# Delta rule attention: the chunk systems stored by column, the solve's operations placed one by one, and another order on all five engines

## The chip, the cores and the metric

One core of a Trainium2 chip runs the whole program. The metric is device microseconds of one execution, the median over runs; lower is better. The kernel runs on five engines with queues of their own: TensorE (PE) for matmuls, VectorE (DVE), ScalarE (ACT), GpSimd (POOL), and SyncE (SP), which here issues the DMAs.

## The reference, cut to what matters

The program is a two-layer decoder (six sub-layers, each followed by a residual sum and a layer norm) on x of shape (2, 2048, 512). The change touches only the first sub-layer, a delta-rule attention with 16 heads of 32 features:

```python
k = _short_conv(x @ Wk.T + bk, wk_conv, bk_conv)   # q and v the same way, 4 taps
beta = jax.nn.sigmoid(x @ Wbeta.T + bbeta)
v = jax.nn.silu(v)
k = k / (knorm + EPS); v = v / (knorm + EPS); q = q / (qnorm + EPS)
def step(S, inp):
    q_t, k_t, v_t, b_t = inp
    pred = jnp.einsum('bhk,bhkv->bhv', k_t, S)
    S = S + b_t[..., None, None] * (k_t[..., None] * (v_t - pred)[..., None, :])
    o_t = jnp.einsum('bhk,bhkv->bhv', q_t, S)
    return (S, o_t)
```

The output is RMS-normalised, goes through `Wo`, is added to x and layer-normed.

## The kernel before, in words

`delta_rule_attention` walks over the sequence in 16 tiles of 128 tokens (both batches at once). Within a tile the recurrence is cut into 4 chunks of 32 tokens. For 32 items (4 head groups x 2 batches x 4 chunks) and the 4 heads in the partitions' quadrants, the triangular 32x32 system of a chunk is inverted in advance, so that the state moves by whole chunks.

A tile n goes through these pieces, each a small function in the code:

- TensorE `project` p = 0 (beta) and 1 to 12 (k, q, v by four groups); ScalarE `keep` (out of PSUM), `first_tap` and `taps` (products of the short convolution); GpSimd `copy_history` and `pair_taps` (L533, sum of two taps); VectorE `join` (L1105, two additions for each of k, q, v), `turn` (L1116, a 32x32 block transpose).
- norms: ScalarE `square` and `take_root`, VectorE `sum_squares` (L1122) and `invert_norms` (L1128 to L1133), GpSimd `rate_keys` (L540) and `mask_beta` (L549).
- the systems: TensorE `keys_keys` (L623), VectorE `mask` (L1143), `to_systems` (L1148: transposes the masked products into `t_sys`), 60 operations `substitute` (L1162 a product, L1165 an addition, each needing the one before), `from_systems` (L1176: transposes back into `tT`), GpSimd `scale_t` (L553).
- the states, for each chunk c: TensorE `predict`, VectorE `miss` (L1186), TensorE `update`, ScalarE `keep_u`, TensorE `step_state`, VectorE `carry` (L1191), then `predict` of the next chunk. `outputs` reads states and `u`.
- the outputs: `square_outputs`, `keep_outputs` (L927), `rms_sum`, `rms_add`, `rms_invert` (L1209 to L1212), `scale_outputs` (L558), `turn_outputs` (L1217), TensorE `project_out` for each batch (L675), VectorE `add` (L1224) and `moments`, `norm.root` on GpSimd, `finish` on ScalarE, `turn_new` and `keep_new`, SP `store`. One PSUM bank, `b_out`, serves `project_out` of both batches and `turn_new`.

The order of the work is written out by hand: on each engine `unrolled` calls `step(n)` for n = 0, 1, ..., and a step names pieces of tile n and of the tiles 1 to 4 before it (`t1` to `t4`). Engines meet only through semaphores, so each engine runs its list strictly in order, and a piece that waits holds all that stand behind it. In the last steps (draining) TensorE and ScalarE also run `next_product` and `keep_next`, first work of the next sub-layer, which otherwise starts when this stage has ended.

The memory that matters: `masked_kq` holds for each of two tile parities, item by item, 32 numbers of the keys' system and 32 of the queries' one after the other. So `to_systems` reads with steps of 64 elements and writes with steps of 32; `from_systems` reads in one run and writes with steps of 32. The products of `substitute` are kept in `squares[:, 0]`, which ScalarE's `square(n, 0)` writes too and therefore waits for the solve.

## Time and profile before

| | |
|---|---|
| median of 3 runs | 2832.5 us (2830.06, 2832.5, 2836.57) |
| span of the profiled execution, first to last instruction | 2826.6 us |
| its own time | not given beside the span; the median lies 5.9 us above the span |
| mean granted TensorE clock | 0.970 of full speed |
| busy over the whole span | PE 90%, DVE 79%, ACT 50%, POOL 18% |
| delta-rule stage | about the first 1041 us of the span |

The page's shares are means over six sub-layers with different limits. The change lies in the first, so the stage's own windows are what counts. "Idle before" in a row of the timeline stands in brackets with the engine that ended it. PE rows of the small matmuls overlap, so a busy PE isn't PE at its peak.

### The profile page before, as it was taken

The page shows a single profiled execution, that of the slowest core. Times are in us where ns is not written, and L with a number is a line of the kernel's source. Part 1 is how long each engine was busy: PE and PEld are TensorE (multiplying, and loading weights), DVE is VectorE, ACT ScalarE, POOL GpSimd, SP SyncE. Part 2 cuts the span into 40 slices and gives each one's busy share as a digit, 9 for nine tenths or more (in the row PEclk, how much of TensorE's full clock was granted, in tenths as well). Part 3 has the DMA queues.
Part 4 walks back from the last instruction along what each step waited for, and adds up shares of the span by engine and source line. Part 5 has one row for each costly group of instructions (what it writes and reads, how often), then busy time and mean ns, then how long its engine had stood idle before and what let it go on. Part 6 is the DMA issues. An engine that isn't in the chain of part 4 may idle for free. (4 is left out here: it accounts for less than half of the span.)

```text
span 2826.6 us, 83010 instructions
## 1 busy us (share of the span) xinstructions
PE 2548.6 (90%) x35304; PEld 1801.5 (64%) x35304; DVE 2224.5 (79%) x4027; ACT 1417.6 (50%) x2569; POOL 512.1 (18%) x661
## 2 busy tenths in 40 slices
PE   6788989899898979999999987997799999989998
PEld 5566666666666756777677654443377777766765
DVE  3898988889998628888887784987778888871886
ACT  7667666777566213323333223545366666651554
POOL 2233322233223210000000000004511111120222
PEclk9999999999999989999999999999899999998999
DMA  2001111111111221121220114548932122123332
GB/s 89 21 16 34 56 34 41 34 34 56 34 41 63 100 97 41 53 75 53 75 68 31 60 60 145 186 158 290 315 118 75 61 61 89 61 75 105 119 121 74
DMA packets 165805, 234.24 MB, mean 83 GB/s; under 512 B 17858, under 2 KB 94018, under 8 KB 162884
## 3 DMA queue, kind: packets, MB, share of 16 engines
q1 hardware_dynamic: 165444, 229.01, 24.6%
q8 instruction: 278, 4.55, 0.7%
q14 instruction: 83, 0.68, 0.1%
HBM read 136.18 MB, written 92.80 MB: 81 GB/s over the span
## 5 line engine op out<-in xcount | busy, mean ns | idle before, releaser
L612 PE MATMUL delta_banks<-both_columns,both_mats 128*128 128x256 f32 x1536 | 383.5, 394 | 5.7 <-ACT both_line L865 4.8
L612 PEld LDWEIGHTS delta_banks<-both_columns,both_mats 128*128 128x128 f32 x1536 | 278.9, 191 | 48.9 <-ACT both_line L865 8.0
L883 ACT ACTIVATE both_product<-both_line,delta_conv_w 128x256 f32<-128x256 f32 x576 | 248.6, 496 | 7.1 <-DVE both_conv L1105 6.2
L1512 PE MATMUL ctxatt_banks<-both_product,ctxatt_oT 128*128 128x512 f32 x512 | 228.4, 599 | 4.9 <-DVE both_conv L1627 4.9
L1473 PE MATMUL ctxatt_banks<-both_line,both_mats 128*128 128x256 f32 x960 | 221.5, 384 | 1.3 <-SPq L1424 1.3
L1473 PEld LDWEIGHTS ctxatt_banks<-both_line,both_mats 128*128 128x128 f32 x960 | 180.5, 193 | 24.8 <-SPq L1424 1.6
L1162 DVE TENSOR_TENSOR delta_squares<-delta_t_sys 128x30 f32<-128x30 f32 (+14 forms) x480 | 175.0, 365 | 12.5 <-issue 0.2
L1165 DVE TENSOR_TENSOR delta_t_sys<-delta_t_sys,delta_squares 128x30 f32<-128x30 f32 (+14 forms) x480 | 165.4, 345 | 16.5
L865 ACT ACTIVATE both_line<-delta_banks,delta_proj_b 128x256 f32<-128x256 f32 x192 | 87.8, 457 | 170.3 <-PE delta_banks L612 170.1
L1512 PEld LDWEIGHTS ctxatt_banks<-both_product,ctxatt_oT 128*128 128x128 f32 x512 | 95.3, 191 | 115.5 <-issue 109.0
L1559 ACT ACTIVATE ctxatt_probsT<-ctxatt_banks 128x512 f32<-128x512 f32 x128 | 69.5, 594 | 189.3 <-PE ctxatt_banks L1494 189.2
L533 POOL TENSOR_TENSOR both_product<-both_product 128x1024 f32<-128x1024 f32 x48 | 116.9, 2437 | 186.8 <-ACT both_product L883 186.8
L675 PE MATMUL delta_banks<-delta_woT,delta_oT 128*128 128x512 f32 x256 | 126.2, 639 | 22.7 <-DVE delta_norm_y L1224 22.7
L2447 PE MATMUL wkv_banks<-wkv_mixed,decay_wkT 128*128 128x256 f32 x512 | 118.3, 386 | 19.1 <-DVE wkv_mixed L2624 11.0
L1105 DVE TENSOR_TENSOR both_conv<-both_conv,both_product 128x1024 f32<-128x1024 f32 x96 | 117.7, 1226 | 19.8 <-POOL both_product L533 15.3
L219 POOL TENSOR_TENSOR ctxatt_norm_var_eps<-ctxatt_norm_moments,ctxatt_eps 128x2 f32<-128x2 f32 x16 | 3.1, 194 | 665.4 <-DVE ctxatt_norm_moments L203 665.4
L2447 PEld LDWEIGHTS wkv_banks<-wkv_mixed,decay_wkT 128*128 128x128 f32 x512 | 96.7, 193 | 42.3 <-issue 18.4
L2456 PE MATMUL wkv_banks<-decay_woT,wkv_oT 128*128 128x512 f32 x256 | 117.7, 604 | 3.7 <-issue 3.7
L1554 ACT ACTIVATE ctxatt_probs<-ctxatt_scores 128x1024 f32<-128x1024 f32 x64 | 67.3, 1051 | 102.3 <-DVE ctxatt_scores L1607 102.3
L2447 PE MATMUL wkv_banks<-wkv_mixed,decay_wrT 128*128 128x256 f32 x512 | 114.0, 381 | 3.6 <-ACT decay_last L2553 3.6
L2447 PE MATMUL wkv_banks<-wkv_mixed,decay_wvT 128*128 128x256 f32 x512 | 115.7, 379 | 0.0
L875 ACT ACTIVATE both_conv<-both_line,delta_conv_b,delta_conv_w 128x256 f32<-128x256 f32 x192 | 112.4, 593 | 4.4 <-DVE delta_v_tok L1116 0.9
(366 smaller groups left out, 5816.6 us busy)
## 6 DMA issues: line engine op xcount, KB each, us to landing
h<-ffn_hid SPq DMA_DIRECT2D x66, 256.0 KB, 2.1
xT<-both_newT SPq DMA_DIRECT2D x24, 512.0 KB, 3.6
x<-both_new SPq DMA_DIRECT2D x24, 512.0 KB, 4.0
x<-decay_last SPq DMA_DIRECT2D x24, 512.0 KB, 7.3
ffn_hid<-h SPq DMA_DIRECT2D x6, 1536.0 KB, 8.3
both_columns<-xT SPq DMA_DIRECT2D x16, 512.0 KB, 4.9
delta_x<-x SPq DMA_DIRECT2D x16, 512.0 KB, 4.0
both_line<-xT SPq DMA_DIRECT2D x16, 512.0 KB, 4.6
```

Of the source, the lines that this page charges most:

```text
L533: pool.tensor_tensor(two_taps, two_taps, last, ALU.add).then_inc(paired, 1)
L612: mm = pe.matmul(b_proj[:, p % 2, 0:B * P], wT[NAMES[i]][:, k, g * P:(g + 1) * P], xT_sb[:, n.parity, k], start=k == 0, stop=k == KB - 1)
L675: mm = pe.matmul(b_out, oT[:, g, b * P:(b + 1) * P], woT[:, g], start=g == 0, stop=g == KB - 1)
L875: act.activation(conv[:, i, g].rearrange("p (b t) -> p b t", b=B), line[:, i, g, :, 0:P], ACT.Identity, bias=conv_b[:, i, g:g + 1], scale= ...
L883: made = act.activation(slot(n, i)[:, j - 1, g].rearrange("p (b t) -> p b t", b=B), line[:, i, g, :, j:j + P], ACT.Copy, scale=conv_w[:, i ...
L1105: c.did(dve.tensor_tensor(total, total, slot(n, i)[:, half_of].rearrange("p g n -> p (g n)"), ALU.add))
L1162: c.did(dve.tensor_tensor(parts, t_sys[:, j + 1:, j:j + 1].to_broadcast([P, rows, j]), t_sys[:, j:j + 1, 0:j].to_broadcast([P, rows, j]), ...
L1165: c.did(dve.tensor_tensor(to, to, parts, ALU.add))
L1473: mm = pe.matmul(b_q[:, i * B * P:(i + 1) * B * P], wq[:, k, pair * P:(pair + 1) * P], xT_sb[n.parity][:, k], start=k == 0, stop=k == KB - 1)
L1512: mm = pe.matmul(b_o[:], oT[:, b, k, :], wo[:, k, :], start=k == 0, stop=k == PAIRS - 1)
L2447: mm = pe.matmul(bank(i, q)[:, j * WCOLS:(j + 1) * WCOLS], mats[name][:, k, u * P:(u + 1) * P], mixed[:, n.parity, i, k].rearrange("p b t ...
L2456: mm = pe.matmul(banks[:, OUT_BANK + r], oT[:, n.parity, k, r * P:(r + 1) * P], mats["woT"][:, k], start=k == 0, stop=k == KB - 1)
```

## The change

- `t_sys` is stored by column instead of by row: `to_systems` and `from_systems` now write in one run and read with steps of 32 elements. `masked_kq` becomes three planes (keys; queries of even tiles; queries of odd tiles), so that the reading step is 32 and not 64.
- `from_systems` writes a new tile `t_raw`, with item and token turned round; `scale_t` on GpSimd reads it with steps of 32 elements and writes `tT`. The wait on `updated` moves from `from_systems` to `scale_t`. `substitute` keeps its products in `t_raw` as well, waits at its first operation for the last tile's `scale_t`, and `square(n, 0)` no longer waits for the solve.
- `solve`, four operations at a time, is gone: each of the 60 stands in the step by itself.
- The lists of all five engines are written in another order. GpSimd, TensorE, ScalarE and SP name tiles up to 5 back; `copy_history` and `taps` get one more wait each that the new order needs.

```diff
-        masked_kq = sb("masked_kq", [P, 2, ITEMS, 2, DD])
+        masked_kq = sb("masked_kq", [P, 3, ITEMS, DD])
+        t_raw = sb("t_raw", [P, DD, ITEMS])
...
                 def copy_history(n, i):
                         wait(pool, taps_made, n, TAP_OPS, (i + 1) * KB - TAP_OPS)
+                        wait(pool, first_made, n, TAP_OPS, (i + 1) * KB - TAP_OPS)
...
                 def scale_t(n):
                     wait(pool, solved, n, SOLVE_OPS, SOLVE_OPS)
-                    pool.tensor_tensor(tT[:], tT[:], rate_of(n), ALU.mult).then_inc(t_scaled, 1)
+                    wait(pool, updated, n, CHUNKS, 0)
+                    pool.tensor_tensor(tT[:], t_raw[:].rearrange("p t i -> p i t"), rate_of(n), ALU.mult).then_inc(t_scaled, 1)
...
                 def square(n, i):
-                        wait(act, solved, n, SOLVE_OPS, 0)
...
                 def to_systems(n):
-                    dve.transpose(t_sys[:].rearrange("p i j -> p j i"), masked_kq[:, n.parity, :, 0].rearrange("p i s -> p s i")).then_inc(systems, 1)
+                    dve.transpose(t_sys[:], masked_kq[:, 0].rearrange("p i s -> p s i")).then_inc(systems, 1)
...
                 def substitute(n, k):
+                    if k == 0:
+                        wait(dve, t_scaled, n, 1, 0)
-                    parts, to = flat(squares[:, 0])[:, 0:rows * j].rearrange("p (i c) -> p i c", i=rows), t_sys[:, j + 1:, 0:j]
+                    parts, to = flat(t_raw[:])[:, 0:rows * j].rearrange("p (c i) -> p c i", c=j), t_sys[:, 0:j, j + 1:]
...
                 def from_systems(n):
-                    wait(dve, updated, n, CHUNKS, 0)
-                    c.did(dve.transpose(tT[:].rearrange("p i t -> p t i"), t_sys[:]))
+                    c.did(dve.transpose(t_raw[:], t_sys[:].rearrange("p j i -> p i j")))
```

The new step of VectorE, in short: turn_beta(t1), carry(t3,0), miss(t3,1), mask(t2,0..1), rms_invert(t4), join(t2,2,1), carry(t3,1), mask(t2,2..3), miss(t3,2), to_systems(t2), turn_outputs(t4), join(t1,0,0), substitute 0 to 19, join(t1,0,1), add(t4,0), turn(t2,2), carry(t3,2), substitute 20 to 24, join(t1,1,0), add(t4,1), 25, join(t1,1,1), 26, moments(t4), 27, miss(t3,3), 28, turn(t1,1), 29 to 42, carry(t3,3), 43 to 51, turn(t1,0), 52, miss(t2,0), 53 to 59, sum_squares(t1,0), from_systems(t2), sum_squares(t1,1), rms_sum(t3), join(t1,2,0), rms_add(t3), invert_norms(t1).

That of TensorE: predict(t3,1), turn_new(t5,1), project(t1,6), update(t3,1), keys_keys(t2,2..3), step_state(t3,1), predict(t3,2), project(t1,7..8), update(t3,2), outputs(t3,0..1), project_out(t4,0), outputs(t3,2), step_state(t3,2), project(t1,9), project_out(t4,1), predict(t3,3), project(t1,10..12), update(t3,3), outputs(t3,3), project(n,0), step_state(t3,3), project(n,1), keys_keys(t1,0..1), predict(t2,0), project(n,2), turn_new(t4,0), project(n,3..4), update(t2,0), step_state(t2,0), project(n,5).

Three places on which the prediction rests. First VectorE behind the solve, in a steady step. The names are the program's: `delta_squares<-both_conv` is `turn` of q, `delta_k_tok` that of k. Before:

```order
L1116 STREAM_TRANSPOSE delta_k_tok<-both_conv 128x1024
L1176 STREAM_TRANSPOSE delta_tT<-delta_t_sys 128x32x32
L1191 TENSOR_TENSOR delta_states<-delta_banks,delta_states 128x256
L1116 STREAM_TRANSPOSE delta_squares<-both_conv 128x1024
L1186 TENSOR_TENSOR delta_missing<-delta_v_tok,delta_banks 128x256
L1122 TENSOR_REDUCE delta_ss<-delta_squares 128x32 x2
L1196 TENSOR_REDUCE delta_o_ss<-delta_o_squares 128x32
L1202 SCALAR_TENSOR_TENSOR delta_o_ss<-delta_q_norm,delta_o_ss 128x32
L1191 TENSOR_TENSOR delta_states<-delta_banks,delta_states 128x256
L1128 RECIPROCAL delta_r<-delta_root 128x64
```

After:

```order
L1178 TENSOR_TENSOR delta_t_sys<-delta_t_sys,delta_t_raw 128x30
L1132 TENSOR_REDUCE delta_ss<-delta_squares 128x32
L1184 STREAM_TRANSPOSE delta_t_raw<-delta_t_sys 128x1024
L1132 TENSOR_REDUCE delta_ss<-delta_squares 128x32
L1204 TENSOR_REDUCE delta_o_ss<-delta_o_squares 128x32
L1115 TENSOR_TENSOR both_conv<-both_conv,both_product 128x1024
L1210 SCALAR_TENSOR_TENSOR delta_o_ss<-delta_q_norm,delta_o_ss 128x32
L1138 RECIPROCAL delta_r<-delta_root 128x64
```

The transpose of k, `carry`, the transpose of q and `miss`, which stood in front of and behind `from_systems`, are gone from here; `rms_sum` and a `join` now stand between `from_systems` and the norms.

Second, VectorE behind `invert_norms`, up to the masks and `rms_invert`. Before:

```order
L1105 TENSOR_TENSOR both_conv<-both_conv,both_product 128x1024
L1186 TENSOR_TENSOR delta_missing<-delta_v_tok,delta_banks 128x256
L1143 TENSOR_TENSOR delta_masked_kq<-delta_banks,delta_weights_kq 128x512 x2
L1182 STREAM_TRANSPOSE delta_beta<-delta_beta_T 128x256
L1105 TENSOR_TENSOR both_conv<-both_conv,both_product 128x1024
L1209 RECIPROCAL delta_o_r<-delta_o_root 128x32
L1210 TENSOR_TENSOR delta_o_r<-delta_o_r,delta_o_ss 128x32
```

After:

```order
L1190 STREAM_TRANSPOSE delta_beta<-delta_beta_T 128x256
L1199 TENSOR_TENSOR delta_states<-delta_banks,delta_states 128x256
L1194 TENSOR_TENSOR delta_missing<-delta_v_tok,delta_banks 128x256
L1154 TENSOR_TENSOR delta_masked_kq<-delta_banks,delta_weights_kq 128x8x2x32 x2
L1217 RECIPROCAL delta_o_r<-delta_o_root 128x32
L1218 TENSOR_TENSOR delta_o_r<-delta_o_r,delta_o_ss 128x32
L1219 TENSOR_TENSOR delta_o_r<-delta_o_r,delta_o_root 128x32
L1220 RECIPROCAL delta_o_r<-delta_o_r 128x32
L1115 TENSOR_TENSOR both_conv<-both_conv,both_product 128x1024
L1199 TENSOR_TENSOR delta_states<-delta_banks,delta_states 128x256
L1154 TENSOR_TENSOR delta_masked_kq<-delta_banks,delta_weights_kq 128x8x2x32 x2
```

`join` (two inputs in SBUF) no longer follows the norms at once; `turn_beta`, `carry(t3,0)` and `miss(t3,1)` do, and `rms_invert` stands right behind the first two masks.

Third, GpSimd from `scale_t` on. Before, from one `scale_t` to the next tile's `rms` sums:

```order
L553 TENSOR_TENSOR delta_tT<-delta_tT,delta_rate 128x1024
L562 TENSOR_TENSOR delta_x<-delta_x,delta_bo_rep 128x1024
L528 COPY both_line<-both_line 128x8x3
L540 TENSOR_TENSOR delta_rate<-delta_r,delta_beta 128x32
L549 TENSOR_TENSOR delta_weights_kq<-delta_masks,delta_rate 128x32x32
L533 TENSOR_TENSOR both_product<-both_product 128x1024 x2
L528 COPY both_line<-both_line 128x8x3 x2
L558 TENSOR_TENSOR delta_o_tok<-delta_o_tok,delta_o_r 128x1024
L533 TENSOR_TENSOR both_product<-both_product 128x1024
L239 TENSOR_TENSOR delta_norm_var_eps<-delta_norm_moments,delta_eps 128x2
```

After, from the two `copy_history` on:

```order
L531 COPY both_line<-both_line 128x8x3 x2
L566 TENSOR_TENSOR delta_x<-delta_x,delta_bo_rep 128x1024
L557 TENSOR_TENSOR delta_tT<-delta_t_raw,delta_rate 128x1024
L543 TENSOR_TENSOR delta_rate<-delta_r,delta_beta 128x32
L552 TENSOR_TENSOR delta_weights_kq<-delta_masks,delta_rate 128x32x32
L536 TENSOR_TENSOR both_product<-both_product 128x1024
L531 COPY both_line<-both_line 128x8x3
L562 TENSOR_TENSOR delta_o_tok<-delta_o_tok,delta_o_r 128x1024
L536 TENSOR_TENSOR both_product<-both_product 128x1024 x2
```

`add_bias` (`delta_x`) now stands in front of `scale_t` and not behind it, and the two `pair_taps` of k and q stand together behind `scale_outputs`.

## Rows read from the trace of the kernel before

**Rows 1.** Busy time by stretch: one steady step, then the draining.
```profile
core 0: us, PE busy (x) PEld busy (x) DVE busy (x) ACT busy (x) POOL busy (x), PEclk, DMA share, GB/s
...
347.24:405.91 58.67, 52.83 (x1664) 39.45 (x1664) 52.78 (x107) 39.71 (x82) 18.30 (x16) 0.97 0.12 40
...
934.20:1000.00 65.80, 56.79 (x1680) 43.84 (x1681) 36.21 (x89) 15.10 (x31) 8.78 (x9) 0.97 0.29 106
```

**Rows 2.** Tile `t_sys`, two of VectorE's instructions: min/median/max ns, first and last start.
```profile
L1148 DVE STREAM_TRANSPOSE delta_t_sys<-delta_masked_kq x16: 2127/2152/2171, 65.2 to 934.2; 128x1024 f32<-128x1024 f32 x16
...
L1176 DVE STREAM_TRANSPOSE delta_tT<-delta_t_sys x16: 1873/1922/1955, 96.8 to 970.2; 128x1024 f32<-128x1024 f32 x16
```

**Rows 3.** Waits of that step: engine line <- who ended it: us, times, longest.
```profile
DVE delta_masked_kq L1143 <- POOL delta_weights_kq L549: 1.9, 1, 1.9
...
DVE both_conv L1105 <- POOL both_product L533: 0.6, 1, 0.6
DVE delta_states L1191 <- PE delta_banks L632: 0.6, 1, 0.6
DVE delta_norm_y L1224 <- PE delta_banks L675: 0.5, 1, 0.5
```

**Rows 4.** Timeline of VectorE, same step: start, duration, instruction.
```profile
356.43 2.36 DVE L1162 TENSOR_TENSOR delta_squares<-delta_t_sys 128x168 f32<-128x168 f32 x1
358.83 0.33 DVE L1165 TENSOR_TENSOR delta_t_sys<-delta_t_sys,delta_squares 128x168 f32<-128x168 f32 x1
...
365.77 0.41 DVE L1162 TENSOR_TENSOR delta_squares<-delta_t_sys 128x238 f32<-128x238 f32 x1
366.21 0.41 DVE L1165 TENSOR_TENSOR delta_t_sys<-delta_t_sys,delta_squares 128x238 f32<-128x238 f32 x1
...
386.87 1.22 DVE L1116 STREAM_TRANSPOSE delta_squares<-both_conv 128x1024 f32<-128x1024 f32 x1
...
394.65 1.16 DVE L1105 TENSOR_TENSOR both_conv<-both_conv,both_product 128x1024 f32<-128x1024 f32 x1
...
401.86 1.99 DVE L1210 TENSOR_TENSOR delta_o_r<-delta_o_r,delta_o_ss 128x32 f32<-128x32 f32 x1
```

**Rows 5.** Timeline of VectorE in the draining, GpSimd at rest.
```profile
931.97 0.19 DVE L1210 TENSOR_TENSOR delta_o_r<-delta_o_r,delta_o_ss 128x32 f32<-128x32 f32 x1
```

**Rows 6.** Timeline of GpSimd around the same steps.
```profile
356.22 2.38 POOL L533 TENSOR_TENSOR both_product<-both_product 128x1024 f32<-128x1024 f32 x1 [8.37 <-ACT both_product L883]
...
386.76 1.92 POOL L553 TENSOR_TENSOR delta_tT<-delta_tT,delta_rate 128x1024 f32<-128x1024 f32 x1 [15.48 <-DVE delta_tT L1176]
388.63 2.37 POOL L562 TENSOR_TENSOR delta_x<-delta_x,delta_bo_rep 128x1024 f32<-128x1024 f32 x1
...
394.81 1.12 POOL L540 TENSOR_TENSOR delta_rate<-delta_r,delta_beta 128x32 f32<-128x32 f32 x1 [3.66 <-DVE delta_r L1133]
396.01 1.91 POOL L549 TENSOR_TENSOR delta_weights_kq<-delta_masks,delta_rate 128x1024 f32<-128x1024 f32 x1
...
401.45 2.36 POOL L533 TENSOR_TENSOR both_product<-both_product 128x1024 f32<-128x1024 f32 x1 [1.21 <-ACT both_product L883]
```

**Rows 7.** Timeline of TensorE, same step, one kind of work a row.
```profile
354.19 3.70 PE L675 MATMUL delta_banks<-delta_woT,delta_oT 128*128 128x512 f32 x8
...
361.81 5.29 PE L675 MATMUL delta_banks<-delta_woT,delta_oT 128*128 128x512 f32 x8 [2.70 <-DVE delta_norm_y L1224]
...
370.17 0.75 PE L632 MATMUL delta_banks<-delta_u,delta_k_tok 32*32 32x32 f32 x64
370.85 1.99 PE L612 MATMUL delta_banks<-both_columns,both_mats 128*128 128x256 f32 x8
```

**Rows 8.** Timeline of ScalarE, same step.
```profile
384.52 1.01 ACT L927 ACTIVATE delta_o_tok<-delta_banks 128x1024 f32<-128x1024 f32 x1
...
386.80 1.06 ACT L912 ACTIVATE delta_squares<-delta_k_tok 128x1024 f32<-128x1024 f32 x1 [0.77 <-DVE delta_tT L1176]
...
389.56 1.30 ACT L883 ACTIVATE both_product<-both_line,delta_conv_w 128x256 f32<-128x256 f32 x3
```

524 lines of the change are left out of this document (291 added, 233 removed).

## The prediction

> **What bounds the kernel now.** I read the windows first. A steady step takes 58.67 us; in it VectorE is busy 52.78 and TensorE 52.83, ScalarE 39.7 and GpSimd 18.3 [rows 1]. So two engines are close to full, and the question is which of them is ever kept waiting. The waits answer it: VectorE idles 1.9 + 0.6 + 0.6 + 0.5 = 3.6 us for others [rows 3] (another 0.2 stands before one addition), and the remaining 58.67 - 52.78 - 3.8 = 2.1 us are the short gaps between dependent operations of the solve. Busy, waits and gaps fill the whole step: **VectorE sets the pace**, TensorE follows with some 6 us of idle time.
>
> VectorE's busy time is itself not all work. The timeline shows a product over 168 elements that takes 2.36 us, though the addition of the same size behind it takes 0.33 [rows 4]; it runs from 356.43 to 358.79, and GpSimd's `pair_taps` from 356.22 to 358.60 [rows 6]. L1210 takes 1.99 us from 401.86 while GpSimd works from 401.45 to 403.81 [rows 4, 6], and 0.19 with GpSimd at rest [rows 5]. A VectorE operation with both inputs in SBUF stands still until GpSimd's tensor operation is over; block transposes, which have one input, keep their 1.22 us. It holds the other way too: `rate_keys`, 32 elements, took 1.12 us because it met a `join` that ran from 394.65 to 395.81 [rows 4, 6]. Two such stalls a step cost 2.03 + 1.80 = 3.8 us.
>
> How often is it paid? `to_systems` starts at 65.2 us for the first tile and at 934.2 for the last [rows 2]: 869 us for 15 intervals, 57.9 each.
>
> **The change on VectorE, per step.**
>
> *Transposes.* `to_systems` takes 2.15 us, `from_systems` 1.92 [rows 2], a transpose in runs on both sides 1.22 [rows 4]. So writing in steps costs 1.92 - 1.22 = 0.70, and reading in steps on top of it 0.23. Reading in steps alone, which both now do, no row shows. If the costs add, it is 1.22 + 0.23 = 1.45; the ends are 1.22 (free) and 2.15 (the slower side hides the other, and reading is the slower). I take 1.45, since `from_systems` shows that writing in steps alone already costs most: -0.70 - 0.47 = -1.2 us; ends -1.6 and +0.2.
>
> *Stalls behind GpSimd.* In the new order `pair_taps` of q should run while VectorE does an addition from PSUM and the transpose of v, and `add_bias` behind the last `substitute`. What remains is `rms_invert`: it follows two masks of 0.6 us each, `pair_taps` of v starts with the first of them and lasts 2.36, so its tensor operation stands 0.8 to 0.9. -3.8 + 0.9 = -2.9; ends -3.8 (none) and 0 (two elsewhere).
>
> *Waits.* All 3.8 us of now stand at places that are gone. Three new ones: `miss(t3,1)` is behind `carry(t3,0)` and needs a `predict` of 0.75 and two hand-overs, +0.9; the masks need `rate_keys` and `mask_beta` after `invert_norms`, which without the `join` take 0.2 + 1.91 + hand-overs = 2.4, of which `turn_beta`, `carry`, `miss` and that wait cover 2.0, +0.4; `carry(t3,1)` needs six pieces of TensorE (below), +0.6. -3.8 + 1.9 = -1.9; ends -3.8 and 0.
>
> *The sixty operations.* A dependent one starts 0.03 us after the end of the one before (366.21 against 365.77 + 0.41), an independent one some 0.08 before the recorded end [rows 4]. The eight runs of now become ten, so two links of 0.11 us each go: -0.2. Their shapes keep their number of elements with inner and outer length exchanged, and run through the same set in reverse: 0. The Trainium skill, page VectorE: DVE Perf Modes, section The DRAIN you can't avoid, holds that a semaphore between chained operations costs nothing; by that the term would be 0, not -0.2, some 3 us over the stage.
>
> *`scale_t`* reads in steps. It takes 1.92 us [rows 6] with whole runs; the same operation with two full inputs 2.37 [rows 6]. Lower end 1.9; upper end 3.3, if it grew as transposes did (2.15 : 1.22). I take 2.4, the nearest row of a dearer input. Behind it a `join` stands about 0.2 longer: +0.2 (0 to +1). The Trainium skill, GPSIMD Engine Reference, section 7. Performance pitfalls for Q7 kernels, says that reads stepping over more than 8 bytes cost half as much again; as an estimate by that page 2.9 us, and 0.5 us a step more than my sum.
>
> Sum for VectorE: -1.2 - 2.9 - 1.9 - 0.2 + 0.2 = -6.0, so **52.7 us** would do.
>
> **The change on TensorE.** It does the same pieces. One of them is dear today: after 2.70 us of waiting for VectorE's addition, `project_out` took 5.29 instead of 3.70 [rows 7]; the granted clock of the step is 0.97 [rows 1], so some 6% of it, 3.5 us, ran at the lower level (1.2 GHz instead of 2.4). In the new order three pieces stand between the two `project_out`, `add(t4,0)` comes in time, and this wait goes. TensorE then needs 52.83 - 1.59 = 51.2 us, plus the waits of the new order. I placed the pieces of one step in order, a projection at 1.9, a chunk's product at 0.7, `keys_keys` at about 1.0 as it has twice the columns [rows 7]:
>
> - `predict(t3,2)` for `carry(t3,1)`: after `carry(t3,0)` at 0.9 us come 0.7 + 0.5 + 1.9 + 0.7 + 2.0 + 0.7 = 6.5 us; state and hand-overs take 0.6 us: 0.6.
> - `outputs(t3,3)`: ScalarE has `keep_kq` and two `keep` in front of `keep_u(t3,3)`: 0.9.
> - `project(n,4)` needs `keep(n,2)`, which ScalarE reaches after the transpose of k, a square (1.06), `taps` twice (1.30 each), `keep_outputs` (1.01) [rows 8] and itself: 5.1 us after the transpose, when TensorE has been ready for 1.7.
> - `update(t2,0)`, `step_state(t2,0)`, `project(n,5)` behind `scale_t`, `keep_u`, `keep(n,3)`: 0.8.
>
> 51.2 + 4.0 = **55.2 us**. The longer one counts: TensorE, with ScalarE in its loop, becomes the bound, 3.5 us less than 58.67. Every other transfer of work is hidden: ScalarE keeps 15 us of idle time and GpSimd over 35. SP's `store` moves in front of its loads; `load_rows` still comes over 15 us before `add_bias`. `add_bias` in front of `scale_t` is hidden as long as it ends with `from_systems`: transpose of k, square 1.06, taps 1.30, `copy_history` 0.2, `add_bias` 2.37, about 5.1 us, against 0.3 + 0.3 + 1.9 + 1.1 + 1.45 = 5.05 on VectorE. This is even; without that cover each us of delay goes into `update(t2,0)`.
>
> **The sum.** 15 intervals x -3.5 = -52 us. Filling and draining have the same pieces, limited by the chain of states; I take 0, ends -5 and +5. The profiled execution has a span of 2826.6 us, so 2774; the median of the runs lies 5.9 above that span. Predicted: 2832.5 - 52.5 = **2780.0 us**, own range 2764 to 2796.
>
> **Rivals.**
>
> *A. VectorE stays the bound, TensorE's waits close.* -6.0 x 15 = -90: 2743. For it: ScalarE has slack, and the 4.0 us are my placing. Against: five separate waits would have to vanish. 0.10.
>
> *B. GpSimd's long operations meet the solve again.* Sixty operations with both inputs in SBUF stand in the step, and each long GpSimd operation that starts in one of their gaps stops VectorE for 2.0 us. The places for `add_bias` and `pair_taps` are exact to some 0.3 us. Two hits add 4.0 to VectorE's 52.7, 56.7, and delay what TensorE waits for, some 57.2 in all: -1.5 x 15 = -22, 2810 (2797 to 2826). 0.22. The Trainium skill, page SBUF — State Buffer, section Who interferes with whom, calls this an exclusive lock in which issue order decides who is stopped; the rows agree on both directions.
>
> *C. The change does not do what it says.* If reading in steps costs as much as writing in steps did, and the waits removed come back elsewhere, the step stays at 58.7: 2832, within 0.2% (5.7 us, about what a measurement of this kernel can tell). 0.07.
>
> *D. Slower: TensorE's clock.* The one long wait of now cost 1.59 us in the work behind it [rows 7]. The new order has four or five places where TensorE waits. If three or more a step are each followed by such a stretch at the lower level, 55.2 + 3 x 1.59 = 60.0 us: +1.3 x 15 = +20, 2852. It decides from 3.5 / 1.59 = 2.2 stretches a step. Against: waits of about 1 us stand in today's step and the granted clock is 0.97 all the same; only `keep(n,2)`'s nears 2 us. 0.14. The Trainium skill, page TensorE: Matmul & The Clock Gate, Part 1, states that the throttled clock is the default and activity releases it; that is this rival's direction.
>
> **How the numbers follow.** The forecast has 0.47, A 0.10, B 0.22, C 0.07, D 0.14. Faster by over 0.2%: 0.47 + 0.10 + 0.22 = 0.79; same 0.07; slower 0.14. The range 2752 to 2834 takes in the forecast with its bounds, B and C, and leaves out D and half of A, 0.19.
>
> **What would show it.** In the changed profile: both system transposes near 1.45 us; L1210's successor under 1.2 us and no `substitute` over 0.5; `scale_t` near 2.4; the step at 55 us with TensorE idle about 4 us and VectorE waiting for TensorE more than for GpSimd; clock 1.00. Wrong: `substitute` operations of 2 us (B), a granted clock below 0.95 (D), `scale_t` over 3 us with `update(t2,0)` waiting, or an interval of `to_systems` above 57.

## The result and the profile after

The changed kernel takes **2999.05 us** (median of 4 runs, 2988.33 to 3007.1), the kernel before on the same chip 2834.36 (4 runs). The ratio is **1.0587, 95% interval 1.0566 to 1.0609**: 5.9% slower, where 1.9% faster was predicted. The span of the profiled execution is 2994.3 us, its mean granted clock 0.935 (before 0.970).

All of it lies in the delta stage. The tile `t_sys` on VectorE, as [rows 2] (engine, operation, count: min/median/max ns, first and last start):

```profile
L1159 DVE STREAM_TRANSPOSE delta_t_sys<-delta_masked_kq x16: 1919/1926/1970, 64.8 to 1101.5; 128x1024 f32<-128x1024 f32 x16
...
L1184 DVE STREAM_TRANSPOSE delta_t_raw<-delta_t_sys x16: 1887/1917/1987, 99.4 to 1148.3; 128x1024 f32<-128x1024 f32 x16
```

Fifteen intervals now last 1036.7 us, **69.1 each** against 57.9: 11.2 x 15 = 168 us. The transposes cost no more than before. The steady stretch of 810 us, by engine (columns as in [rows 1]), before and after:

```profile
120.00:930.00 810.00, 716.40 (x23026) 540.28 (x23024) 720.90 (x1461) 540.38 (x1099) 250.99 (x200) 0.98 0.12 39
```

```profile
120.00:930.00 810.00, 643.17 (x19250) 496.09 (x19252) 582.38 (x1226) 455.90 (x931) 201.93 (x167) 0.89 0.09 31
```

VectorE is busy 89% of the stretch before and 72% after, so no engine is full any more. The clock fell from 0.98 to 0.89. The waits of that stretch after (us in total, times, longest; "issue" has no releaser that the profile shows):

```profile
DVE delta_states L1199 <- PE delta_banks L636: 69.6, 27, 4.7
DVE delta_norm_y L1232 <- PE delta_banks L679: 65.2, 22, 9.5
DVE delta_missing L1194 <- PE delta_banks L636: 53.4, 25, 4.3
PE delta_banks L636 <- issue: 47.2, 42, 2.1
...
PE delta_banks L636 <- POOL delta_tT L557: 33.5, 11, 4.4
...
PE delta_banks L665 <- issue: 26.3, 13, 4.5
...
PE delta_banks L667 <- issue: 26.2, 13, 4.8
```

VectorE waits for TensorE (188 us in these three rows), TensorE for `scale_t` and for itself. A table of TensorE's whole interval sums this up; each entry is the row's time in the 810 us, scaled by the interval (69.1/810 and so on), and the runs below are in it:

| us per interval | before | after | TensorE spread | before, two pieces early | after, two late | all moves, late |
|---|---|---|---|---|---|---|
| interval | 57.9 | 69.1 | 68.6 | 63.4 | 65.9 | 64.2 |
| busy | 51.2 | 54.9 | 54.5 | 54.7 | 54.1 | 53.9 |
| idle, "issue" (all rows) | 3.5 | 9.7 | 5.8 | 2.3 | 9.6 | 6.7 |
| waiting for `scale_t` | 0 | 2.9 | 7.1 | 4.1 | 0.7 | 2.5 |
| other idle time | 3.2 | 1.6 | 1.1 | 2.3 | 1.5 | 1.1 |

What these entries are is seen in one step. TensorE behind `scale_t` (start, duration, instruction, idle before and who ended it):

```profile
441.91 0.74 PE L636 MATMUL delta_banks<-delta_missing,delta_tT 32*32 32x32 f32 x64 [1.13 <-POOL delta_tT L557]
443.22 0.61 PE L636 MATMUL delta_banks<-delta_u,delta_k_tok 32*32 32x32 f32 x48 [0.57 <-ACT delta_u L902]
445.67 0.44 PE L636 MATMUL delta_banks<-delta_u,delta_k_tok 32*32 32x32 f32 x16 [1.84 <-issue]
446.04 3.78 PE L616 MATMUL delta_banks<-both_columns,both_mats 128*128 128x256 f32 x8
449.75 1.08 PE L636 MATMUL delta_banks<-delta_states,delta_kqT 32*32 32x32 f32 x64
```

`update(t2,0)` waits 1.13 us for `scale_t`; `step_state` halts in the middle of its 64 matmuls for 1.84 us; then `project(n,5)` takes 3.78 us, where the same eight matmuls take 1.99 at the full clock [rows 7], so it ran at the lower level (1.2 instead of 2.4 GHz; the granted clock from 446.04 to 449.75 is 0.50). `predict(t3,1)` behind them is late by all of it. VectorE 60 us later, in the last substitutes, and GpSimd beside it:

```profile
502.24 0.23 DVE L1175 TENSOR_TENSOR delta_t_raw<-delta_t_sys 128x108 f32<-128x108 f32 x1
504.14 0.42 DVE L1194 TENSOR_TENSOR delta_missing<-delta_v_tok,delta_banks 128x256 f32<-128x256 f32 x1 [1.67 <-PE delta_banks L636]
504.48 0.26 DVE L1178 TENSOR_TENSOR delta_t_sys<-delta_t_sys,delta_t_raw 128x108 f32<-128x108 f32 x1
504.78 0.24 DVE L1175 TENSOR_TENSOR delta_t_raw<-delta_t_sys 128x84 f32<-128x84 f32 x1
505.06 2.47 DVE L1178 TENSOR_TENSOR delta_t_sys<-delta_t_sys,delta_t_raw 128x84 f32<-128x84 f32 x1
...
509.55 1.96 DVE L1184 STREAM_TRANSPOSE delta_t_raw<-delta_t_sys 128x1024 f32<-128x1024 f32 x1
```

```profile
505.05 2.37 POOL L566 TENSOR_TENSOR delta_x<-delta_x,delta_bo_rep 128x1024 f32<-128x1024 f32 x1
511.59 2.48 POOL L557 TENSOR_TENSOR delta_tT<-delta_t_raw,delta_rate 128x1024 f32<-128x1024 f32 x1 [4.17 <-DVE delta_t_raw L1184]
```

`miss(t2,0)` stands between substitutes 52 and 53 and waits 1.67 us for TensorE's `predict(t2,0)`; `add_bias` then stops a substitute for 2.2 us (2.47 against 0.26); `from_systems` and `scale_t` come after both. Of the steps between 120 and 930 us, seven have such a stopped substitute; in six of these `update(t2,0)` waits 4.1 to 4.4 us for `scale_t`, in the seventh, shown here, 2.6, and where none is stopped 1.1 to 1.7.

### The profile page after: what moved, and what is told of

Read it like the earlier page. It is cut to its first block and busy times, and to the rows that moved or that the text cites. A ratio compares the mean times of both kernels' runs of the same rounds, so it can differ in the third digit from the quotient of the medians.

```text
span 2994.3 us, 83071 instructions
## 1 busy us (share of the span) xinstructions
PE 2605.1 (87%) x35304; PEld 1859.4 (62%) x35304; DVE 2208.4 (74%) x4027; ACT 1413.5 (47%) x2569; POOL 508.6 (17%) x661
## 5 line engine op out<-in xcount | busy, mean ns | idle before, releaser
L616 PE MATMUL delta_banks<-both_columns,both_mats 128*128 128x256 f32 x1536 | 413.9, 425 | 20.1 <-ACT both_line L866 17.7
L616 PEld LDWEIGHTS delta_banks<-both_columns,both_mats 128*128 128x128 f32 x1536 | 315.3, 213 | 77.9 <-ACT both_line L866 23.7
L1175 DVE TENSOR_TENSOR delta_t_raw<-delta_t_sys 128x30 f32<-128x30 f32 (+14 forms) x480 | 174.9, 364 | 13.8
L1178 DVE TENSOR_TENSOR delta_t_sys<-delta_t_sys,delta_t_raw 128x30 f32<-128x30 f32 (+14 forms) x480 | 166.0, 346 | 13.8
L1619 ACT ACTIVATE ctxatt_probsT<-ctxatt_banks 128x512 f32<-128x512 f32 x128 | 69.5, 594 | 189.2 <-PE ctxatt_banks L1554 189.1
L536 POOL TENSOR_TENSOR both_product<-both_product 128x1024 f32<-128x1024 f32 x48 | 115.6, 2408 | 210.8 <-ACT both_product L885 210.7
L679 PE MATMUL delta_banks<-delta_woT,delta_oT 128*128 128x512 f32 x256 | 141.3, 703 | 0.9 <-DVE delta_norm_y L1232 0.9
L1115 DVE TENSOR_TENSOR both_conv<-both_conv,both_product 128x1024 f32<-128x1024 f32 x96 | 124.7, 1299 | 22.6 <-ACT both_conv L876 19.0
L665 PE MATMUL delta_banks<-delta_states,delta_kqT 32*32 32x32 f32 x4096 | 87.2, 199 | 41.5 <-issue 29.6
L667 PE MATMUL delta_banks<-delta_u,delta_masked_kq 32*32 32x32 f32 x4096 | 87.5, 198 | 36.7 <-issue 36.7
```

Source lines behind the costliest of these rows:

```text
L536: pool.tensor_tensor(two_taps, two_taps, last, ALU.add).then_inc(paired, 1)
L616: mm = pe.matmul(b_proj[:, p % 2, 0:B * P], wT[NAMES[i]][:, k, g * P:(g + 1) * P], xT_sb[:, n.parity, k], start=k == 0, stop=k == KB - 1)
L679: mm = pe.matmul(b_out, oT[:, g, b * P:(b + 1) * P], woT[:, g], start=g == 0, stop=g == KB - 1)
L1115: c.did(dve.tensor_tensor(total, total, slot(n, i)[:, half_of].rearrange("p g n -> p (g n)"), ALU.add))
L1175: c.did(dve.tensor_tensor(parts, t_sys[:, 0:j, j:j + 1].to_broadcast([P, j, rows]), t_sys[:, j:j + 1, j + 1:].to_broadcast([P, j, rows]), ...
L1178: c.did(dve.tensor_tensor(to, to, parts, ALU.add))
```

## The experiments

Seventeen kernels were run, all beside the kernel before on the same chip. "Interval" is (last - first start of `to_systems`)/15.

### The layout, and TensorE's list

**The kernel before with the new layout alone**: `masked_kq`, `t_raw`, `scale_t`, `substitute` and the two transposes as in the change, all lists old.

> The kernel before with the new memory layout alone (both system transposes write in runs and read in steps, scale_t reads in steps, three planes of masks), every order as before. Theory I (TensorE runs out of instructions where the new order puts its groups of small matmuls side by side): the layout is innocent, 2825 to 2845 us; from the changed kernel's rows the transposes give back 0.2 us a step and scale_t takes 2.5 instead of 1.9, hidden. Theory L (the strided reads are the loss): over 2900 us.

Measured 2830.59 against 2831.21, ratio 1.0000 (0.9985 to 1.0016). The layout costs and brings nothing that can be seen; what the change did to the time it did by order (its two additional waits are in the runs with the new lists).

**The changed kernel, small groups apart.** The gaps without releaser fall where `step_state`, `predict`, `keys_keys` and `outputs` stand side by side in the new list, 64 to 256 short matmuls each. Five moves set a long piece between them:

```diff
 keys_keys(t2, 2)
+project(t1, 7)
 keys_keys(t2, 3)
...
 outputs(t3, 0)
-outputs(t3, 1)
 project_out(t4, 0)
+outputs(t3, 1)
+project(t1, 9)
 outputs(t3, 2)
...
 keys_keys(t1, 0)
+project(n, 2)
 keys_keys(t1, 1)
...
-project(n, 4)
 update(t2, 0)
+project(n, 4)
 step_state(t2, 0)
```

> The changed kernel with five pieces of TensorE's list moved so that a projection or an output product stands between groups of small matmuls (keys_keys 2 and 3, outputs 0, 1 and 2, keys_keys 0 and 1, update 0 and step_state 0); nothing else. Theory I: TensorE's idle time before small matmuls that no semaphore explains falls from about 11 us a step to under 5, the clock rises from 0.87, and the time falls by 60 us or more, to 2940 or less. Theory C (the other engines' orders hold TensorE back, its own list is innocent): within 25 us of 2999.

Measured 2989.89, 1.0556 (1.0538 to 1.0575): 9 us. The issue idle fell from 114 to 69 us in the stretch, yet the interval from 69.1 to 68.6 only, since the wait for `scale_t` rose from 33.5 to 84.4:

```profile
PE delta_banks L636 <- POOL delta_tT L557: 84.4, 11, 8.1
```

Part of that rise is GpSimd's: 23 substitutes are stopped in this stretch against 7 in the changed kernel, two a step, one by `pair_taps` (2.30 us at 405.48, beside L536 from 405.25) and one by `add_bias` (2.45 at 439.10, beside L566 from 439.09). Both stand in front of `from_systems`.

**The same in the kernel before, the other way**: three swaps that put small groups side by side.

```diff
-project_out(t4, 0)
 outputs(t3, 1)
+project_out(t4, 0)
...
 update(t2, 0)
-turn_new(t4, 1)
 step_state(t2, 0)
+turn_new(t4, 1)
...
-keys_keys(t1, 2)
 project(n, 6)
+keys_keys(t1, 2)
 keys_keys(t1, 3)
```

> The kernel before with three swaps in TensorE's list that put small groups side by side (keys_keys 2 with 3, outputs 0 with 1, update 0 with step_state 0); every piece within two places of where it stood. Theory I: each pair costs a stall of 1.5 to 2 us somewhere in the step, of which some is hidden, so 2860 to 2920 us, with idle pieces of 1.5 us in the middle of a group. Theory C: within 12 us of 2834.

Measured 2861.58, 1.0111 (1.0085 to 1.0136): +30 us, issue idle 49 to 78, clock 0.96. Packing small groups does cost, but not 168 us.

**Whole lists exchanged.** First the changed kernel with TensorE's list of before; then the kernel before with the new layout and the new lists of VectorE and GpSimd.

> The changed kernel with TensorE's list of the kernel before (in the first draining step the four products of the next sub-layer stand a little earlier, since ScalarE's list asks for them); all else as changed. Theory I (groups of small matmuls side by side run TensorE out of instructions): the stalls go, 2780 to 2850 us. Theory C (VectorE's, ScalarE's and GpSimd's lists make a longer loop with each other whatever TensorE's list is): 2930 or more.

Measured 3043.37, 1.0747 (1.0722 to 1.0772), with issue idle of only 23 us. So TensorE's list alone is not the cause.

> The kernel before with the new layout and the new lists of VectorE and GpSimd; TensorE, ScalarE and SP as before. Theory I: no stall in a group, VectorE gains what its list promises, 2760 to 2840 us. Theory C: over 2900 us, with VectorE waiting for TensorE.

Measured 3098.04, 1.0933 (1.0912 to 1.0955).

**Four of the five moves** (`update(t2,0)` left where the change put it):

> The changed kernel with four of the five moves of e2 in TensorE's list: update 0 stays behind project 4, so that the 7.7 us wait for scale_t that e2 showed is covered again. Theory I: the stalls that stay are those of update 0 with step_state 0 alone, 2900 to 2950 us. If the wait for scale_t was only moved, not made, by e2: again 2985 or more, and then the length of the loop through from_systems and scale_t is a cause of its own.

Measured 2995.0, 1.0579 (1.0556 to 1.0603); issue idle 77, wait for `scale_t` 56 us.

### Which loop is it?

Each gain on TensorE is eaten by the wait for `scale_t`. That wait is the end of a chain that begins on TensorE itself. Where does it leave TensorE? The first guess was `add(t4,0)`, before which VectorE waits up to 9.5 us.

```diff
+substitute(t2, 20) ... substitute(t2, 29)
 join(t1, 0, 1)
 add(t4, 0)
 turn(t2, 2)
 carry(t3, 2)
-substitute(t2, 20) ... substitute(t2, 29)
```

> The changed kernel with one move on VectorE: substitutes 20 to 29 stand ahead of join(t1,0,1), add(t4,0), turn(t2,2) and carry(t3,2) instead of behind them (the pieces between 24 and 34 follow in their old order). Theory C (a closed loop through VectorE's list: from_systems, scale_t, update0, TensorE's list up to project_out 0, add 0, then the rest of the solve up to from_systems): ten substitutes (about 3.4 us) leave the loop and fill the 3.67 us in which VectorE stands before add 0. The interval falls by 3 to 3.5 us, 15 of them 45 to 55 us: 2945 to 2955. Rival I (TensorE's own list, its issue gaps and its slow clock are the bound, VectorE only follows): within 5 us of 2999, the idle time before add 0 goes to another of VectorE's waits. Rival, halfway: TensorE takes over as the bound after 1 or 2 us a step: 2970 to 2985.

Measured 3006.61, 1.0624 (1.0586 to 1.0663). No gain: the wait before `add` fell from 65 to 24 us, those before `carry` rose from 70 to 82, and the interval stayed (69.5). The test isn't clean, since the substitutes now met GpSimd more often (18 stopped instead of 7, about 2 us an interval).

**GpSimd: `scale_t(t4)` first**, ahead of `copy_history(t2,2)` and `add_bias(t5)`:

> The changed kernel with one move on GpSimd: scale_t(t4) ahead of copy_history(t2,2) and add_bias(t5). Theory C: the addition of the bias no longer slows a substitute (2.3 us a step of the solve's last stretch were seen), unless it meets another operation; scale_t itself started only 0.3 us late. Interval shorter by 0 to 2.5 us: 2962 to 2999, middle 2980. Rival I (TensorE bound): 2999 within 5. If copy_history 2, which now waits behind scale_t, makes project and taps late, slower: up to 3020.

Measured 2979.23, 1.0526 (1.0487 to 1.0565): 20 us back by the medians, 17 by the ratios, the middle of what was expected. No substitute is stopped any more in the stretch.

**The five moves of TensorE, ten substitutes earlier, `scale_t` first:**

> The changed kernel with all moves at once: the five of TensorE's list that take small groups apart, substitutes 20 to 29 ahead of add 0, scale_t first on GpSimd. Theory C: TensorE's faster chain (about 3 us a step by the issue time that the first of these moves saved) is no longer eaten by the wait for scale_t, and 3 to 3.5 of VectorE's and up to 2 of GpSimd's come on top: interval 69 down to 61 to 63, 2885 to 2925. Rival I: only the TensorE moves count, 2985 to 2995.

Measured 2995.81, 1.0586 (1.0544 to 1.0628): nothing. The issue idle is down to 79 us, and TensorE waits mainly at one place, 5.5 us for `scale_t` in nearly every step (61 us in the stretch). `add_bias` stops nothing here. The place is seen best in the run with the five moves alone; TensorE, then VectorE, then GpSimd:

```profile
437.65 0.76 PE L636 MATMUL delta_banks<-delta_states,delta_kqT 32*32 32x32 f32 x64
438.35 0.66 PE L689 MATMUL delta_banks<-delta_ident,both_new 128*128 128x128 f32 x4
438.84 1.89 PE L616 MATMUL delta_banks<-both_columns,both_mats 128*128 128x256 f32 x8
448.45 1.08 PE L636 MATMUL delta_banks<-delta_missing,delta_tT 32*32 32x32 f32 x64 [7.72 <-POOL delta_tT L557]
449.46 3.78 PE L616 MATMUL delta_banks<-both_columns,both_mats 128*128 128x256 f32 x8
```

```profile
438.46 0.42 DVE L1196 TENSOR_TENSOR delta_missing<-delta_v_tok,delta_banks 128x256 f32<-128x256 f32 x1 [1.86 <-PE delta_banks L636]
...
439.10 2.45 DVE L1177 TENSOR_TENSOR delta_t_raw<-delta_t_sys 128x84 f32<-128x84 f32 x1
...
443.85 1.89 DVE L1186 STREAM_TRANSPOSE delta_t_raw<-delta_t_sys 128x1024 f32<-128x1024 f32 x1
```

```profile
445.83 2.48 POOL L557 TENSOR_TENSOR delta_tT<-delta_t_raw,delta_rate 128x1024 f32<-128x1024 f32 x1 [4.38 <-DVE delta_t_raw L1186]
```

`predict(t2,0)` ends at 438.41 on TensorE. `miss(t2,0)` waits for it (1.86 us) **inside the solve**; seven substitutes, `sum_squares`, `from_systems` and `scale_t` follow, and only then may `update(t2,0)` start, at 448.45. That is 10.0 us, of which 2.2 are the substitute that `add_bias` stopped, and TensorE has 2.3 of work between the two. This arc closes TensorE's list on itself: whatever TensorE loses between `update(t2,0)` and the next `predict(t2,0)`, to a gap or to a slow clock, VectorE cannot make good, though it is idle a quarter of the time. In the kernel before, `carry(t3,3)` and `miss(t2,0)` stand behind `from_systems`, and `scale_t` waits for no `predict(t2,0)`. (One piece in front of `from_systems` does wait for TensorE there too: `turn(t1,0)` writes the keys' buffer that `step_state(t3,3)` reads.) Four runs test this, two from each side. They move `carry(t3,3)` and `miss(t2,0)` together, so the share of each isn't separated.

**The kernel before with the arc**, nothing else changed:

```diff
 solve(t2, 12)
+carry(t3, 3)
 solve(t2, 13)
+miss(t2, 0)
 solve(t2, 14)
 turn(t1, 0)
 from_systems(t2)
-carry(t3, 3)
 turn(t1, 1)
-miss(t2, 0)
```

> The kernel before with two pieces of VectorE moved and nothing else: carry(t3,3) ahead of solve 13, miss(t2,0) ahead of solve 14, where both stood behind from_systems. Theory E (closed loop over predict 0): miss(t2,0) inside the solve makes from_systems, scale_t and so update 0 wait for TensorE's predict 0, which ends near 447.7 in the step from 405.9, while from_systems now starts at 444.6. miss, the last four substitutes (about 1 us), the transpose of k (1.2 us) and from_systems then come after it: from_systems starts at about 450.3, update 0 about 5 us later than now; the interval grows by 4 to 5.7 us, 15 of them 60 to 85 us: 2890 to 2917. Rival N (no such loop: VectorE has 58 us of work and waits, the 3 us of waiting at miss 0 are made good elsewhere): within 15 of 2831.

Measured **2904.27**, 1.0249 (1.0228 to 1.027): +75 us from two operations of 0.4 us, interval 63.4 where 61.9 to 63.6 was expected. GpSimd's stops are as before (10 substitutes in the stretch, 11 before), so they don't explain it. VectorE and TensorE in one step, and TensorE's wait, which was not among the waits before:

```profile
415.71 0.42 DVE L1186 TENSOR_TENSOR delta_missing<-delta_v_tok,delta_banks 128x256 f32<-128x256 f32 x1 [3.17 <-PE delta_banks L632]
418.04 1.87 DVE L1176 STREAM_TRANSPOSE delta_tT<-delta_t_sys 128x1024 f32<-128x1024 f32 x1
```

```profile
422.04 0.83 PE L632 MATMUL delta_banks<-delta_missing,delta_tT 32*32 32x32 f32 x64 [3.51 <-POOL delta_tT L553]
```

```profile
PE delta_banks L632 <- POOL delta_tT L553: 52.6, 12, 4.5
```

**The changed kernel without it**: `carry(t3,3)` from behind substitute 42 to behind 51, `miss(t2,0)` from behind 52 to behind `from_systems`.

> The changed kernel with two pieces of VectorE moved and nothing else: miss(t2,0) behind from_systems, carry(t3,3) from behind substitute 42 to behind substitute 51. Theory E: in the changed kernel update 0 waits 2.4 us a step for scale_t, and miss 0 waits 0 to 1.7 us for predict 0; both go, but TensorE's issue gaps and the slow clock after them stay: interval shorter by 1 to 2.5 us, 2960 to 2985. Rival N: 2999 within 5.

Measured **2948.22**, 1.0422 (1.0401 to 1.0444): 51 us back, more than the 14 to 39 expected. The wait for `scale_t` is 8.0 us in the stretch, was 33.5; the issue idle stayed (118). No substitute is stopped any more either, which counts into the 51: the run with `scale_t` first, where none is stopped either, got 20 back.

**With the five moves of TensorE and `scale_t` first as well:**

> The changed kernel with the five moves of TensorE's list (its order was dense there: one wait of 7.7 us a step, for scale_t), scale_t first on GpSimd, miss(t2,0) behind from_systems and carry(t3,3) behind substitute 51; add 0 stands where the change put it. Theory E: predict 0, miss 0, the last substitutes, from_systems, scale_t, update 0 is the arc that closes TensorE's loop (8.6 us against 2.6 us of TensorE's own work between predict 0 and update 0); opened, the wait for scale_t falls from 7.7 to 1 to 3 us a step, and project 5 behind it runs at the full clock: interval 69 down to 62 to 64, 2890 to 2925. Rival N: 2980 to 2995, as with TensorE's moves alone.

Measured **2923.52**, 1.0322 (1.0304 to 1.0339), near the upper end; 66 us less than TensorE's moves alone, which alone had brought 9. `scale_t` first is in these 66. The nearer comparison is the run before with TensorE's moves, ten substitutes earlier and `scale_t` first (2995.81): `add_bias` stops nothing in either, `pair_taps` one substitute a step in both (12 and 13 in the stretch), and the late `carry(t3,3)` and `miss(t2,0)` make 72 us, less what the ten substitutes do.

**The kernel before with VectorE's new list alone**, and the same with `carry(t3,3)` and `miss(t2,0)` directly behind `from_systems`:

> The kernel before with the new layout and the new list of VectorE; TensorE, ScalarE, GpSimd and SyncE keep their old lists. The run with both new lists of VectorE and GpSimd took 3098. Theory C (VectorE's list carries the loss): over 3000, most of the 3098. Rival P (GpSimd's new list, with pair_taps and add_bias at its front, carries it): within 20 of 2831. Both share: 2900 to 2990.

Measured 3083.0, 1.0879 (1.0835 to 1.0922): nearly as much as with GpSimd's new list too (3098), so VectorE's list makes most of this loss.

> The kernel before with the new layout and the new list of VectorE, in which now carry(t3,3) and miss(t2,0) stand directly behind from_systems, as they do before the change. With the new list as it was, carry 3 waited 6.3 to 7.0 us in each step and carry 2 6.5 to 9.6 us. Theory E: the wait of carry 3 goes, the one of carry 2 stays; interval shorter by 5 to 7 us, 3083 down to 2980 to 3010. Rival N: over 3060, the waiting goes over to carry 2.

Measured 3071.78, 1.0846 (1.0828 to 1.0864). Missed: 11 us, not 70 to 100. The wait for `scale_t` is gone (60 us to 0) and that of `carry` fell (192.5 to 122.9), but others took their place. On VectorE the transpose of k, `turn(t1,0)`, now waits for `step_state(t3,3)`, in front of `from_systems` as `carry(t3,3)` did:

```profile
DVE delta_states L1196 <- PE delta_banks L635: 122.9, 21, 9.6
...
DVE delta_k_tok L1119 <- PE delta_banks L635: 34.0, 10, 3.7
DVE delta_r L1131 <- issue: 21.5, 10, 2.6
```

On TensorE `predict(t2,0)` waits for `carry(t3,3)` behind `from_systems`; the view calls this idle time "issue" though it is a wait (VectorE, then TensorE):

```profile
472.50 1.93 DVE L1181 STREAM_TRANSPOSE delta_t_raw<-delta_t_sys 128x1024 f32<-128x1024 f32 x1
474.36 0.38 DVE L1196 TENSOR_TENSOR delta_states<-delta_banks,delta_states 128x256 f32<-128x256 f32 x1
```

```profile
474.83 1.08 PE L635 MATMUL delta_banks<-delta_states,delta_kqT 32*32 32x32 f32 x64 [4.19 <-issue]
```

Such pieces, in front of a whole `predict` and right behind a `carry`, are 57 of this run's 79 us of issue idle (0.3 of 24 without the late pieces). In the runs of the table they are 4 to 9 us in the stretch; nearly all the rest stands in the middle of a group, where the code waits for no semaphore. So the arc through `miss(t2,0)` is one of several between the two lists, and opening it gains only where it ends last.

### The rest, and what bounds the kernel before

**The changed kernel with VectorE's operations in the old order**:

> The changed kernel with VectorE's operations in the order of before (sixty single substitutes in the places of the old groups of four, carry 3 and miss 0 behind from_systems, carry and miss of the first chunks at the step's end); the layout and the lists of TensorE, ScalarE, GpSimd and SyncE stay new. Theory L (most of the loss sits in where VectorE's new list puts pieces that wait for TensorE and ScalarE; the kernel before with that list alone took 3083): 2840 to 2900, the rest being TensorE's small groups side by side (30 us in the kernel before). Rival M (the new lists of the others are as much at fault, each fits only to the whole): over 2950.

Measured 3068.23, 1.0835 (1.0811 to 1.086). Rival M holds: exchanging VectorE's list alone makes it worse from either side (3083 against 2831, 3068 against 2999), exchanging TensorE's from the changed side, the only one run (3043 against 2999). The new lists need one another, and together they are still slower than the old ones. Here too 57 of the 149 us of issue idle are `predict` behind `carry`.

**TensorE's outputs as before the change**, in the run of all moves:

```diff
 update(t3, 2)
+project(t1, 9)
 outputs(t3, 0)
 project_out(t4, 0)
 outputs(t3, 1)
-project(t1, 9)
+project_out(t4, 1)
 outputs(t3, 2)
 step_state(t3, 2)
-project_out(t4, 1)
```

> The run of all moves with the late miss 0 and carry 3 (2923), and on TensorE the outputs as before the change: project 9 between update 2 and outputs 0, project_out 1 between outputs 1 and outputs 2. There a gap of 3.9 us without releaser stood in outputs 0, and project_out 0 behind it took 6.6 us instead of 3.7. Theory I as a part (gaps where small groups meet, and the slow clock behind them): 1.5 to 3 us a step, 2878 to 2905. Rival: the wait for scale_t takes it over, 2915 to 2930.

Measured 2954.81, 1.0418 (1.0396 to 1.0441): 31 us slower than without it. The gaps shrank (85 to 75 us), but `step_state(t3,2)` came later, and `carry(t3,2)`, in front of the last forty substitutes, waited 3.5 to 9.0 us for it in the stretch instead of 0.6 to 5.6.

**The kernel before with `turn_beta(t1)` and `rms_invert(t4)` ahead of the masks:**

> The kernel before with one move on VectorE: turn_beta(t1) and rms_invert(t4) ahead of mask(t2,0..1), out of the 1.9 us for which the masks wait for GpSimd, and out of the way of pair_taps 2. If VectorE's list bounds the kernel before: the 1.8 us in which L1210 stood still and up to 1.2 us of small operations go, 1.5 to 3 us a step, 2785 to 2810. If TensorE bounds it (issue gaps and its own waits, 57 of 58 us): 2825 to 2835.

Measured 2870.3, 1.0129 (1.0109 to 1.0149): 37 us slower, outside both expectations. VectorE, then TensorE:

```profile
412.60 0.35 DVE L1209 RECIPROCAL delta_o_r<-delta_o_root 128x32 f32<-128x32 f32 x1 [0.99 <-ACT delta_o_root L931]
...
413.21 2.22 DVE L1211 TENSOR_TENSOR delta_o_r<-delta_o_r,delta_o_root 128x32 f32<-128x32 f32 x1
...
415.74 1.22 DVE L1143 TENSOR_TENSOR delta_masked_kq<-delta_banks,delta_weights_kq 128x512 f32<-128x512 f32 x2
```

```profile
416.63 1.13 PE L623 MATMUL delta_banks<-delta_kqT 32*32 32x64 f32 x64 [3.80 <-DVE delta_masked_kq L1143]
417.69 3.60 PE L612 MATMUL delta_banks<-both_columns,both_mats 128*128 128x256 f32 x8
```

`rms_invert` waited 0.99 us for its root and was then stopped for 2 us by `pair_taps`, which ran from 413.00 to 415.39. The masks came late, TensorE's `keys_keys` waited 3.80 us (15.8 us in the stretch before, 48.3 now), and the `project` behind it took 3.60 instead of 1.99. A delay of VectorE is paid on TensorE, and some of it twice. So it is not VectorE's busy time alone that paces the kernel before. No version beat it.

## Why the prediction was wrong

*The bound.* "VectorE sets the pace" rested on busy time, waits and short gaps that fill the step [rows 1, 3]. They do. But TensorE's interval was as full, and I hadn't split its idle time: of 57.9 us, 51.2 are busy, **3.5 are "issue" idle**, 3.2 are waits and short gaps. The run with the masks late (+37 us) shows that TensorE has little slack there.

*The step that failed: "51.2 + 4.0 = 55.2".* Its parts, as measured: waits 4.5 (2.9 for `scale_t` and 1.6) against 4.0, right in size by luck, since `project(n,4)` waited 0.2 instead of 1.7 and the wait for `scale_t`, one part of a term of 0.8, became 2.9; busy 54.9 against 51.2; issue idle 9.7 against nothing. Even by the kernel before, 3.5 belonged into the sum, which then gives 58.7, no gain at all. (The step that I took, 58.67 us, was 0.7 longer than the mean interval of 57.9, which alone made 3.5 of a gain of 2.7.) The new list put small groups side by side and made it 9.7; the reverse test gives 30 us for three such pairs.

*Clock.* 51.2 was the work at the higher level throughout. "Clock 1.00" became 0.89, and 3.7 us more of busy time an interval. Rival D had this direction and missed the cause: I counted waits of the list, not gaps, as what a slow stretch follows. The Trainium skill, TensorE: Matmul & The Clock Gate, Part 1, which stood behind that rival, is borne out in direction: a wait or gap is followed by work at 1.2 GHz (3.78 behind a gap of 1.84 with waits of 1.13 and 0.57 ahead of it; 3.60 behind 3.80; 3.78 behind 7.72; at the full clock 1.99).

*The loop.* I placed a step from one end to the other and let VectorE and TensorE each take "the longer one". That `miss(t2,0)` now stands in front of seven substitutes and `from_systems` is in the rows on order and in no term. It makes TensorE's list wait for itself. With it a gap isn't hidden behind VectorE's slack of 20 us but paid in full: putting it into the kernel before costs 75 us, taking it out of the changed one gives 51, or 66 where the gaps are reduced and `scale_t` comes first too. These are not parts of one sum, since the gaps, the stopped substitutes and the arc lengthen the same loop. With VectorE's new list in the kernel before it gave 11, as other waits between the same two lists took over.

*Transposes*: 1.45 was wrong; reading in steps costs what writing in steps did (1.93 and 1.92), so -0.2 instead of -1.2 us.

*`scale_t`*: 2.48 measured, 2.4 taken.

```profile
L557 POOL TENSOR_TENSOR delta_tT<-delta_t_raw,delta_rate x16: 2470/2480/2493, 101.4 to 1150.3; 128x1024 f32<-128x1024 f32 x16
```

The 2.9 us estimated from the Trainium skill's GPSIMD Engine Reference were too high here: the reading in steps cost 29% (2.48 against 1.92), not half as much again, and the measurement decides.

*The dependent links* (-0.2) are too small to be told apart in any run.

*Stalls behind GpSimd*: largely right. In 120 to 930 us the kernel before has 24 (11 substitutes, 13 L1210 or L1211), the changed one 7, all substitutes and none at `rms_invert`: 1.2 us an interval, where 0.9 was forecast.

*`add_bias` "is even"*: it took the time that I gave it, from the end of the transpose of k at 502.3 to 507.4, 5.1 us, and `scale_t` behind it on GpSimd did not wait for it. But `miss(t2,0)` had waited 1.67 us, so the last five substitutes were still to come at 505.05, and it stopped one for 2.2 us. In the step before, `miss(t2,0)` did not wait (434.05) and none was stopped. That is rival B, one hit in seven of the stretch's steps. Moving `scale_t` ahead of it gave 20 us. The lock that the Trainium skill's page SBUF — State Buffer describes shows again in both places (2.47 and 2.22 us for operations of 0.26 and 0.19).

*Waits of VectorE*: 1.9 forecast, in the step from 414.5 to 484.0 5.8 + 5.8 + 4.8 + 1.4 = 17.8, all behind TensorE and ScalarE, as one expects of an engine that no longer sets the pace.

*What stays open.* The run with all moves is still 94 us above the kernel before. By the table it has 6.3 us more an interval: 2.7 busy (clock), 3.2 issue idle, 2.5 `scale_t`, 2.1 less of other waits. That names where the time is, not an order that removes it; the one attempt made it worse. A substitute a step is still stopped by `pair_taps` in it (about 2 us each), which no run took out. What halts TensorE in a gap was not tested by itself. The trace shows where it happens. The changed kernel has 44 gaps of over 1.3 us between 120 and 930, and each stands a whole number (1 to 10) times 126.5 to 128 matmuls behind the one before. In one pair of `outputs` two follow each other, with 128 matmuls between:

```profile
613.34 0.23 PE L667 MATMUL delta_banks<-delta_u,delta_masked_kq 32*32 32x32 f32 x5 [1.72 <-issue]
...
619.42 0.33 PE L667 MATMUL delta_banks<-delta_u,delta_masked_kq 32*32 32x32 f32 x8 [4.78 <-issue]
```

So a gap goes by the count of TensorE's instructions, 128 matmuls with their 128 weight loads, and not by a semaphore. In the step above the DMA view from 440 to 450, in 40 slices of 0.25 us, has two instruction packets, one at 442.75 to 443.0 and one at 447.5:

```profile
GB/s 0 0 0 0 0 0 0 0 0 0 0 66 0 0 0 0 0 0 0 0 0 0 0 0 0 0 0 0 0 0 66 0 0 0 0 0 0 0 0 0
...
q8 instruction: 2, 0.03, 1.6%
```

The gap runs from 443.83 to 445.67, behind the first. By the Trainium skill, Runtime: NRT & Kernel Launch, section Instruction fetch mechanics, engines fetch in blocks of 256 instructions, at a cost that is mostly hidden. The gaps, if they are this, are not hidden here. The step has 13 packets on that queue, and the 1664 matmuls of a step [rows 1] with as many weight loads are 13 x 256 instructions. Small groups side by side use up such a block in some 1.5 us (64 matmuls of them take 0.75), a long piece has sixteen instructions in 1.99. That fits the count and the two placing experiments. That gaps fall at the ends of blocks of this length is shown; that the fetch is what is waited for is argued, not shown.

## What to carry to other kernels

When operations are moved between engines' lists, don't compare each engine's sum; close the loop. Follow a tile's chain until it comes back to the engine it left, and add what that engine does in between at the clock and with the gaps that its own rows show. A short operation that waits for another engine must not stand in front of the work that this engine waits for in turn. There can be several such arcs between two lists, and opening one helps only where it ends last. And split an engine's idle time into waits and issue gaps before calling the rest slack.
